# Graph layer with residual and layer norm: six of sixteen tiles of each sort batch go through memory by GpSimd scatters

## The reference

```python
messages = einsum('ei,oi->eo', x[dst], W) + b
agg = segment_sum(messages * agg_weight, src, num_segments=100000)
out = layernorm(x + agg)          # over the 128 features, eps 1e-5
```

## Time and profile before

| | us |
|---|---|
| median of 3 executions (lowest, highest) | 994.42 (992.21, 997.78) |
| the profiled execution | 992.53 |
| its span, first to last instruction | 990.8 |
| busy: TensorE / VectorE / ScalarE / GpSimd | 886.5 / 854.7 / 726.0 / 476.4 |

### The profile page before, as it was taken

The page is one execution under the profiler, slowest core; times in us unless marked ns, Lnnn a source line. Parts: engine busy times, 40 slices in busy tenths (PEclk is TensorE's granted clock), DMA queues, the critical chain, the costliest instruction groups (busy, mean ns, idle before and its releaser), DMA issues.

```text
span 990.8 us, 26454 instructions
## 1 busy us (share of the span) xinstructions
PE 886.5 (89%) x7344; PEld 723.1 (73%) x7344; DVE 854.7 (86%) x3787; ACT 726.0 (73%) x1896; POOL 476.4 (48%) x513
## 2 busy tenths in 40 slices
PE   2649999999999579999999898989898989898996
PEld 2635555555555368889889797979797979797995
DVE  7958989989989858979798989989697979797997
ACT  0016576676676348879798897979697979798998
POOL 2010000000000077777777777777677777777771
PEclk9989999999999879999999999999899999999999
DMA  2001111111110137767677777878676767676784
GB/s 69 2 2 64 64 46 44 65 44 44 65 44 24 43 86 217 221 192 234 199 225 207 222 224 202 241 200 225 182 236 200 229 191 235 206 222 201 223 240 157
DMA packets 77596, 149.48 MB, mean 151 GB/s; under 512 B 15412, under 2 KB 16448, under 8 KB 77488
## 3 DMA queue, kind: packets, MB, share of 16 engines
q1 hardware_dynamic: 61808, 116.20, 36.7%
q0 software_dynamic: 15680, 32.14, 13.6%
HBM read 96.95 MB, written 51.33 MB: 150 GB/s over the span
## 4 chain that ended last, share of the span: by engine, by line
PE 57%; DVE 28%; issue 9%; ACT 4%; DMA 1%; DVEq 1%; POOL 1%; ACTq 0%; SPq 0%; POOLq 0%
PE bank L556 16%; PE bank L604 14%; PE bank L614 12%; DVE stats L833 7%; DVE sel L820 6%; DVE h L827 4%; PE bank L601 3%; DVE oh_hi L665 3%; PE bank L500 3%; DVE mv L839 3%; PE bank L516 3%; PE bank L616 2%; PE bank L519 2%; ACT y L917 2%; PE bank L530 1%
## 5 line engine op out<-in xcount | busy, mean ns | idle before, releaser
L452 POOL DMA_INDIRECT xg<-in_x,now x490 | 467.7, 954 | 436.1 <-DVE now L812 293.9
L917 ACT ACTIVATE y<-h,shift,rstd 128x128 f32<-128x128 f32 x784 | 320.2, 479 | 0.1
L614 PE MATMUL bank<-wT,aggT 128*128 128x128 f32 x1568 | 290.4, 308 | 33.3 <-ACT deg L907 33.3
L604 PE MATMUL bank<-sel,xg 128*128 128x269 f32 (+5 forms) x1370 | 288.5, 352 | 22.1 <-DMA xg<-in_x,now 18.2
L614 PEld LDWEIGHTS bank<-wT,aggT 128*128 128x128 f32 x1568 | 242.3, 195 | 48.8 <-ACT deg L907 36.1
L604 PEld LDWEIGHTS bank<-sel,xg 128*128 128x128 f32 x1370 | 235.6, 198 | 51.8 <-issue 24.9
L820 DVE TENSOR_SCALAR sel<-iota_win,now 128x269 f32<-128x269 f32 (+1 forms) x490 | 156.5, 370 | 25.7 <-PE bank L601 25.5
L616 PE MATMUL bank<-b,deg 128*128 128x128 bf16 x784 | 174.2, 222 | 0.0
L556 PE MATMUL bank<-oh_t,oh_s 128*128 128x490 bf16 x782 | 173.8, 369 | 0.0
L833 DVE BATCH_NORM_STATS2 stats<-h 128x6 f32<-128x128 f32 x784 | 168.9, 277 | 0.2
L827 DVE SCALAR_TENSOR_TENSOR h<-bank,aw,xt 128x512 f32<-128x512 f32 x196 | 147.1, 751 | 16.6 <-issue 10.5
(11 more groups left out here) (128 smaller groups left out, 687.3 us busy)
## 6 DMA issues: line engine op xcount, KB each, us to landing
xt<-in_x SPq DMA_DIRECT2D x195, 256.0 KB
out<-y SPq DMA_DIRECT2D x195, 256.0 KB
hi_row<-hi_scratch SPq DMA_DIRECT2D x25, 512.0 KB, 3.7
xg<-in_x,now POOLq DMA_INDIRECT x490
src_rows<-in_src SPq DMA_DIRECT2D x1, 192.0 KB
dst_rows<-in_dst SPq DMA_DIRECT2D x1, 192.0 KB
hi_scratch<-hi_rows SPq DMA_DIRECT2D x1, 128.0 KB, 2.0
xt<-in_x SPq DMA_DIRECT2D x1, 80.0 KB
```

What stands on the lines that cost most here:

```text
L452: nc.gpsimd.indirect_dma_start(out=xg[:, m, k], out_offset=None, in_=x, in_offset=bass.IndirectOffsetOnAxis(ap=now[:, m, k, 0:1], axis=0)) ...
L604: nc.tensor.matmul(AGG[q][:, at:at + hi - lo], xg[:, ring, k], sel[:, half, k, lo:hi], start=(i == 0), stop=(i == len(parts) - 1), skip_gr ...
L614: nc.tensor.matmul(OUT[u][:, nodes], aggT[:, q, nodes], wT[:], start=(j == 0), stop=False, skip_group_check=True)
L917: nc.scalar.activation(y[:, u, j], h[:, u, j], ACT.Identity, bias=shift[:, u, j:j + 1], scale=rstd[:, u, j:j + 1]).then_inc(s_y, 1)
```

## The change

- **Six of 16 tiles.** Of each batch but the last two only 10 tiles go through one-hots and TensorE (13 of batch 23, all 7 of batch 24), 250 of 391. For the other 141, VectorE works out one row number per edge (`linear`, `place_row`: slot times 490 plus chunk), and GpSimd writes the edge's two words (8 bytes, now side by side in `word_col`) with an indirect DMA of 128 rows into `place_scratch` in memory. SyncE blanks that memory ahead of the loop and reads it back to `scattered` after the last scatter. `keep` and `dump` send the rows elsewhere in the slow path.
- **Order on TensorE.** The tiles of the batch before are placed in parts of 2, 3 and 5. In batch 0, `same` 0 and 1 stand ahead of `prefix`, and the transpose of the maximum is a product of a widened column.
- **Start.** The first two one-hots of `hi` stand ahead of the counts, the bias steps in the wait for the first small DMA, the reciprocal of the first 64 columns in the wait for the second, and that of the other 448 inside batch 1.
- **End.** The table in memory is joined to those in PSUM by OR. ScalarE copies the second table from PSUM. The first 20 columns are decoded first, their four `now` copies follow, and then the other 470 columns. VectorE loads the flag of the branch before it waits for the tables.

The diff, cut to its core (new semaphores, names of counts and the slow path's waits are left out):

```diff
+    BY_PE = [10] * (B - 2) + [13, C - (B - 1) * BC]
+    SCATTERS = C - sum(BY_PE)
...
+        word_col = sb("word_col", [P, KB * P, 2])
+        w1_col, w2_col = word_col[:, :, 0], word_col[:, :, 1]
...
+        place_row = sb("place_row", [P, B, BC], i32)
+        linear = sb("linear", [P, BC])
+        keep = sb("keep", [P, 1])
+        dump = sb("dump", [P, B, BC])
+        most_wide = sb("most_wide", [HI, P])
+        scattered = sb("scattered", [P, NB, 2])
...
-            second(B - 1, (B - 1) % 2, 0, C - (B - 1) * BC)
+            second(B - 1, (B - 1) % 2, 0, BY_PE[B - 1])
+        def part_of(k, quarter):
+            if k == 0:
+                return 0, 0
+            cuts = (0, BY_PE[k - 1] // 4, BY_PE[k - 1] // 2, BY_PE[k - 1])
+            return cuts[quarter], cuts[quarter + 1]
+        def before_tile(k, i):
+            return sum(BY_PE[:k]) + i
@@ sync @@
+            blank = place_scratch[0:P * NB].rearrange("(p t) w -> p (t w)", p=P)
+            sp.wait_ge(s_blank, 1)
+            sp.dma_start(blank, scattered[:].rearrange("p t w -> p (t w)")).then_inc(s_blanked, 16)
...
+            sp.wait_ge(s_scatter, 16 * SCATTERS)
+            sp.dma_start(scattered[:].rearrange("p t w -> p (t w)"), blank).then_inc(s_scattered, 16)
@@ gpsimd @@
+            nc.gpsimd.memset(scattered[:], 0.0).then_inc(s_blank, 1)
...
+            nc.gpsimd.iota(dump[:].rearrange("p k c -> p (k c)"), [[P, CA]], base=P * NB, channel_multiplier=1,
+                           allow_small_or_imprecise_dtypes=True).then_inc(s_const, 1)
...
+            pool.wait_ge(s_blanked, 16)
+            for k in range(B - 1):
+                pool.wait_ge(s_row, k + 1)
+                pool.nop(nofuse=True)
+                for i in range(BY_PE[k], BC):
+                    nc.gpsimd.indirect_dma_start(
+                        out=place_scratch, out_offset=bass.IndirectOffsetOnAxis(ap=place_row[:, k, i:i + 1], axis=0),
+                        in_=word_col[:, k * BC + i], in_offset=None).then_inc(s_scatter, 16)
@@ tensor @@
-            pe.wait_ge(s_mx, 1)
-            nc.tensor.transpose(SORT[1][0:1, 0:HI], most_hi[:], ident[0:HI, 0:HI]).then_inc(s_mxT, 1)
...
-                prefix()
+                if k:
+                    prefix()
                 pe.wait_ge(s_hiT, k + 1)
                 same(0)
                 same(1)
-                place_some(0, 4)
+                if k == 0:
+                    prefix()
+                    pe.wait_ge(s_mx, 1)
+                    nc.tensor.matmul(SORT[1][:, 0:HI], most_wide[:], ident[0:HI, 0:HI], start=True, stop=True).then_inc(s_mxT, 1)
+                place_some(*part_of(k, 0))
                 pe.wait_ge(s_bnow, k + 1)
                 at_least(pe, s_own, k - 1)
+                if k == 1:
+                    pe.wait_ge(s_over, 1)
                 add(0)
                 same(2)
                 add(1)
                 same(3)
-                place_some(4, 8)
+                place_some(*part_of(k, 1))
                 add(2)
                 add(3).then_inc(s_q, 1)
-                place_some(8, BC)
+                place_some(*part_of(k, 2))
@@ vector @@
-            dve.wait_ge(s_cvt, 6)
-            after(V.reciprocal(ratio_col[:], w1_col[:]))
-            V.tensor_tensor(ratio_col[:], w2_col[:], ratio_col[:], ALU.mult).then_inc(s_zero, 1)
+            def first_hots(k):
+                dve.wait_ge(s_hrow[k], 16)
+                V.tensor_scalar(oh_hiT[:, k], hi_row[:, k], part[:], None, ALU.is_equal).then_inc(s_hiT, 1)
+            first_hots(0)
+            first_hots(1)
...
+            dve.wait_ge(s_cvt, 6)
+            early = 4 * BC
+            after(V.reciprocal(ratio_col[:, 0:early], w1_col[:, 0:early]))
+            V.tensor_tensor(ratio_col[:, 0:early], w2_col[:, 0:early], ratio_col[:, 0:early], ALU.mult).then_inc(s_ratio, 1)
+            dve.wait_ge(s_spilled, 16)
...
+            V.tensor_scalar(most_wide[:], ones[0:HI], most_hi[:], None, ALU.mult).then_inc(s_mx, 1)
...
+            def rank(k, q, hots_some):
+                if k > 1:
+                    dve.wait_ge(s_hrow[q], 16 * (k // 2) + 16)
+                    dve.wait_ge(s_q, k - 1)
+                    V.tensor_scalar(oh_hiT[:, q], hi_row[:, q], part[:], None, ALU.is_equal).then_inc(s_hiT, 1)
+                if k == 0:
+                    dve.wait_ge(s_mxT, 1)
+                    after(V.tensor_reduce(most_all[:], SORT[1][:, 0:HI], AX, ALU.max))
+                    V.tensor_scalar(over[:], most_all[:], float(most), None, ALU.is_gt).then_inc(s_over, 1)
+                    V.tensor_scalar(keep[:], most_all[:], float(most), None, ALU.is_le)
+                    after(V.tensor_scalar(most_all[:], most_all[:], float(most), None, ALU.is_gt))
+                    after(V.tensor_scalar(dump[:], dump[:], most_all[:], None, ALU.mult))
+                hots_some(0, BY_PE[k - 1] if k else 0)
+                if k == 1:
+                    after(V.reciprocal(ratio_col[:, early:], w1_col[:, early:]))
+                    V.tensor_tensor(ratio_col[:, early:], w2_col[:, early:], ratio_col[:, early:], ALU.mult
+                                    ).then_inc(s_ratio, 1)
+                dve.wait_ge(s_q, k + 1)
+                V.tensor_tensor(own[:], SORT[q][:, 0:BC * LO].rearrange("p (c l) -> p c l", l=LO),
+                                oh_lo[:, k], ALU.mult).then_inc(s_own, 1)
+                dve.wait_ge(s_own, k + 1)
+                V.tensor_reduce(place_at[:], own[:], AX, ALU.add).then_inc(s_place_at, 1)
+                dve.wait_ge(s_place_at, k + 1)
+                V.tensor_scalar(beyond[:], place_at[:], float(P), float(P), ALU.is_ge, ALU.mult).then_inc(s_beyond, 1)
+                dve.wait_ge(s_beyond, k + 1)
+                V.scalar_tensor_tensor(slot[:, q], place_at[:], float(2 * P - 1), beyond[:], ALU.min, ALU.subtract
+                                       ).then_inc(s_slot, 1)
+                V.scalar_tensor_tensor(t_now[:, q], beyond[:], 1.0 / P, t_col[:, k * BC:(k + 1) * BC], ALU.mult, ALU.add
+                                       ).then_inc(s_slot, 1)
+                if k < B - 1:
+                    dve.wait_ge(s_slot, 2 * k + 2)
+                    V.scalar_tensor_tensor(linear[:], slot[:, q], float(NB), t_now[:, q], ALU.mult, ALU.add
+                                           ).then_inc(s_linear, 1)
+                    dve.wait_ge(s_linear, k + 1)
+                    V.scalar_tensor_tensor(place_row[:, k], linear[:], keep[:], dump[:, k], ALU.mult, ALU.add).then_inc(s_row, 1)
...
+            lagging(rank, spread)
+            dve.wait_ge(s_over, 1)
+            flag = dve.value_load(over[0:1, 0:1], min_val=0, max_val=1)
+            dve.wait_ge(s_place, C - SCATTERS)
+            dve.wait_ge(s_scattered, 16)
             i1, i2 = tab1.bitcast(i32), tab2.bitcast(i32)
-            V.tensor_scalar(emp, i1, FULL, FULL, XOR, AND)
-            V.tensor_scalar(low4, i2, 15 << 25, 25, AND, LSR)
-            after(V.tensor_scalar(tabi[:], i1, 8191 << 16, 12, AND, LSR))
-            after(V.tensor_tensor(low4, low4, tabi[:], OR))
-            after(V.tensor_scalar(tabi[:], emp, 30, None, LSR))
-            after(V.scalar_tensor_tensor(table[:, :, 0], tabi[:], part[:], low4, ALU.mult, ALU.add))
-            after(V.tensor_scalar(emp, emp, 20, None, LSR))
-            after(V.tensor_scalar(tabq[:], i2, (GN - 1) << 16, 16, AND, LSR))
-            after(V.tensor_tensor(table[:, :, 1], tabq[:], emp, OR))
-            flag = dve.value_load(over[0:1, 0:1], min_val=0, max_val=1)
+            other1, other2 = (scattered[:, :, w].bitcast(i32) for w in range(2))
+            V.tensor_tensor(i1, TABLES[0][:, 0:NB].bitcast(i32), other1, OR).then_inc(s_dec1, 1)
+            dve.wait_ge(s_dec1, 1)
+            dve.wait_ge(s_dec2, 1)
+            def decode(lo, hi):
+                c = slice(lo, hi)
+                after(V.tensor_tensor(i2[:, c], i2[:, c], other2[:, c], OR))
+                V.tensor_scalar(emp[:, c], i1[:, c], FULL, FULL, XOR, AND)
+                V.tensor_scalar(low4[:, c], i2[:, c], 15 << 25, 25, AND, LSR)
+                after(V.tensor_scalar(tabi[:, c], i1[:, c], 8191 << 16, 12, AND, LSR))
+                after(V.tensor_tensor(low4[:, c], low4[:, c], tabi[:, c], OR))
+                after(V.tensor_scalar(tabi[:, c], emp[:, c], 30, None, LSR))
+                after(V.scalar_tensor_tensor(table[:, c, 0], tabi[:, c], part[:], low4[:, c], ALU.mult, ALU.add))
+                after(V.tensor_scalar(emp[:, c], emp[:, c], 20, None, LSR))
+                after(V.tensor_scalar(tabq[:, c], i2[:, c], (GN - 1) << 16, 16, AND, LSR))
+                after(V.tensor_tensor(table[:, c, 1], tabq[:, c], emp[:, c], OR))
+            head = 5 * (RX // 2)
...
+            decode(0, head)
...
+                for pair in range(RX // 2):
+                    V.tensor_copy(now[:, pair].rearrange("p k w -> p (k w)"),
```

(68 more changed lines are left out.)

68 lines of the change are left out of this document (27 added, 41 removed).

## The result

The changed kernel takes 954.16 us (median of 4 runs, 952.67 to 957.55), the kernel before 996.1 in the same comparison: ratio 0.9579, interval 0.9551 to 0.9607. The forecast was 922 with a range of 915 to 940, so the time lies 14 us above the range. The profiled execution has a span of 950.8 us.

The account below looks back on a forecast made before the run. It took TensorE to pace the sort loop, with 645.0 us of main loop unchanged. From 992.53 us it subtracted 10.3 (start), 55.5 (loop) and 5.2 (end), 71.0 in all, giving 921.5, stated as 922, range 915 to 940.

Parts of the forecast that it names:

- the first part: Account of what bounds the kernel: TensorE paces the sort loop; the main loop's 645.0 us stay, its rounds untouched.
- the five cases: The forecast outcome (chance 0.70) and four rivals: late GpSimd, VectorE bound, scatters blocked, start not shortened.
- Tiles off TensorE, the whole loop: Sort loop: six tiles fewer cut a batch from 10.57 to 8.11 us, the loop from 251.8 to 196.3, 55.5 less.
- The start: Ahead of the sort loop: reordered steps bring `own` of batch 0 to 68.35, 10.3 us earlier.
- The end: Last `own` to first gather: 10.2 us instead of 15.35, 5.2 us less; later main loop costs at most 0.3.
- The scatters: Sort loop on GpSimd: 1.29 us per scatter, hidden behind the placements, cost nothing, 2 us in hand.
- bound 1.37: Break-even time per scatter in us, at which the read back lands with the sort's last placement.
- GpSimd late: Rival in the sort: a scatter costs between 1.37 and 1.6 us; 1.5 gives 940 us in total; chance 0.10.
- the prediction's formula: Read back's landing: 71.2 - 0.3 + 141 X + 5.8, X us per scatter, set against last placement at 270.35.
- VectorE as the bound: Rival in the sort: VectorE's tile steps stretch beside GpSimd, a batch takes 8.6 us, total 933; chance 0.10.
- Blocked scatters: Rival from `place_row` to the read back: GpSimd stalls during VectorE's tile and `hi` steps, total 1038 us; chance 0.05.
- The start that doesn't shorten: Rival ahead of or early in the sort: counts or TensorE wait for something else, 10 us less gain, 932; chance 0.05.

Follow-up runs that it names:

- a_noscat_r: Changed kernel without scatters, all tiles through TensorE, loop body moved to place 3 by 14 idle instructions: 971.69 us, ratio 0.9764.
- a_pad40: Changed kernel with 40 idle instructions in VectorE's never-taken branch, moving the loop body to place 3: 917.77 us, ratio 0.9206.
- a_moved_r: Changed kernel with GpSimd's long memsets moved later, body at place 3: 913.89 us, ratio 0.9189; on a slow chip, iota moved too, 1351.7 us, ratio 1.0279.
- a_by8_r: Changed kernel with eight tiles of sixteen scattered in place of six, body at place 3 by 4 idle instructions: 968.0 us, ratio 0.9723.
- b_pad82_r: Kernel before the change with 82 idle instructions, body at place 3: 981.35 us, ratio 0.9857; on a slow chip 1300.65 us, ratio 0.9926.
- a_span12: Changed kernel with SPAN 12 instead of 4, a loop body three times as long with 2 jumps back instead of 10: 918.9 us, ratio 0.9217.

## Why the prediction was wrong

**The step that failed** is this one, of the first part: "nothing in the edit touches its rounds", and, in the end, "So 645 us of main loop follow the first gather as before; cost at most 0.3 us". The instructions of the rounds are untouched, but the edit moved them in VectorE's program, from place 49 to 91, and the loop took 674.0 us. Padding alone, in either kernel, makes 672.5 to 675.1 us out of it, or 633.3 to 637.5. With 674.0 in the sum in place of 645.0 the forecast would have been 951, and 954.16 was measured. None of the five cases contained it: all looked into the sort, and the range was made of theirs. The 4 us at each of 10 turns stood in the trace of before, as 41 us of waits at `now`; I had read over them, as something that would stay. That "faster" came true is no merit of this part: the gain of the sort was large enough to bear 29 us of loss.

The Trainium skill has the rule that bears on it, in "Runtime: NRT & Kernel Launch", section "Instruction fetch mechanics": a taken branch whose target lies outside the window of loaded instructions makes the sequencer fetch it before it goes on. The runs agree, with 6 to 7 us a turn at place 91 and none at place 3. On sizes they differ: the section has the instructions refilled in blocks of 16 KiB, 256 instructions, and here the packets on VectorE's queue are of 8 KiB and the stalls are the same again 128 instructions on.

The other steps:

- *Tiles off TensorE, the whole loop.* 8.11 us forecast for a steady batch, 8.08 measured; 196.3 for the loop, 196.31 measured. a_noscat_r shows that it comes from there. The last digit is luck: the first two batches and the last took 0.1 to 0.2 us more each than forecast and the others 0.5 less in all, and in a_pad40, with the same steps, the loop took 197.8.
- *The start.* Forecast 68.35 for `own` of batch 0, measured 70.78. "GpSimd's new memset and iota ... nothing" was wrong in a way that I didn't look for: not that someone waits for them, but that a GpSimd memset holds VectorE's own small steps. Before the change the memset of `xg` fell into the time of VectorE's reciprocal; now it falls on `origin`. a_moved_r gives back 2.3 us, 0.9 of them ahead of `origin`.
- *The end.* 10.2 us from the last `own` to the first gather forecast, 9.67 measured.
- *The scatters.* 1.29 us each, taken from the gathers, bound 1.37: measured 1.325 by a_by8_r, which leaves 0.045 us a scatter in place of 0.08. In the changed kernel it is less: GpSimd starts 1.1 us behind `place_row` in most batches, stands still once for 2.98 us ("issue", before the scatter at 230.09), and from then on runs back to back, 3.8 us behind, at 1.34 us a scatter, 8.06 a batch of 8.08, so that it can't catch up. The read back was issued at 268.68 and takes 3.4 us; the last placement ended at 272.8. So 0.7 us were in hand, not 2, and the cost was nothing.
- *The rivals.* GpSimd late: not here, but a_by8_r is that situation brought about with 46 scatters more. By the prediction's formula 187 scatters of 1.325 us land and are read back at 324.5, some 70 us behind the last placement; VectorE waited 72. VectorE as the bound: no, TensorE is busy for all of the stretch above. The start that doesn't shorten: no. Blocked scatters, the rule of the Trainium skill in "SBUF — State Buffer", section "Who interferes with whom": on this chip no, since 1.325 to 1.34 us against the 1.25 of undisturbed gathers is 6 to 7%. The same section has the lock both ways, whoever issues first blocking the other, and it is the other way that cost: GpSimd's memset, issued first, held VectorE's cast. That it was by this lock is not shown.
- *The main loop at the same place* is 637.5 us in a_pad40 and 633.3 in b_pad82_r. The 490 gathers that pace it take 963 ns in the one and 954 in the other, 4.2 us of busy time in all, which is the difference. Why they do isn't settled.

## What to carry over

When an edit changes how many instructions stand ahead of a hardware loop, count the packets of the instruction queues at a turn before and after (a sum over the kernel can mislead, see a_span12) and look at the first steps of each turn: if VectorE stands still there with nothing shown that it waits for, a few idle instructions in a branch never taken can be worth more than the next tuning step, here 36 us of 954. Stalls of that kind are not linear in what they cost: in the main loop 41 us of them cost 12 (645.0 against 633.3), 65 cost 37 (674.0 against 637.5). Two things in the traces can be behind that, and no run separates them: the slack that VectorE has beside the gathers, and TensorE's low clock, 3.4 us behind most turns in the one case and 6.8 in the other. And a split of work between two engines should be costed at the point where the second one saturates: six scatters a batch gained 54 us, eight gained 4.

## What I had not expected of the hardware

- A loop of 331 VectorE instructions runs with no instruction load at its turns at some places and with five packets a turn at others; the two differ by 36 us of 954.
- A stall of VectorE at a turn is followed by a stretch of TensorE at half its clock, 6.8 us at 0.50 at the end of 5.68 us of idle time and behind it. With the stalls gone (a_pad40) the clock is 1.00 from 330 to 900 us.
- GpSimd's memset of 128x2560 float32 (2.23 us) stopped three VectorE steps of 64x8 until it ended, 1.25 to 1.40 us each in place of 0.15 to 0.17. VectorE's large integer steps at 5.6 and 6.3 us took 0.73 and 1.39 beside GpSimd's iota and memsets, 0.50 and 0.43 in a_moved_r.
- A scatter of 128 rows into memory takes 0.97 us of GpSimd and 0.30 to the next, hardly more than a gather, but 42 of the 141 in the changed kernel take 1.13 or 1.26.
- On two other chips the same kernels take a third longer (1312 and 1332 us for the kernel before), on the one whose kernels can be compared it is the main loop (951.9 us in b_pad82 in place of 633.3) and the sort with scatters that take longer, the sort without scatters not at all, and the change in its best version is a loss of 3% there (a_moved against before). A gain that rests on GpSimd's indirect DMAs should be measured on more than one chip.
